# The row maximum of the third stage as a bias of the exponentials, one per head

## The reference

```
h = layernorm(x, ln1_g, ln1_b)
qkv = (h @ Wqkv).reshape(B, S, 16, 24)
q, k, v = qkv[..., :8], qkv[..., 8:16], qkv[..., 16:]
q, k = (rope(q), rope(k))
scores = einsum('bqhd,bkhd->bhqk', q, k) / sqrt(8)
scores = where(causal, scores, -1e9)
probs = softmax(scores, axis=-1)
attn = einsum('bhqk,bkhd->bqhd', probs, v).reshape(B, S, 128) @ Wproj
x = x + attn
```

## Time and profile before

| what | value |
|---|---|
| runs of the kernel before | 4290.12, 4294.4, 4306.48 us; median 4294.4 |
| profiled execution | 4309.58 us, its span 4307.5 us |
| mean granted clock of TensorE | 0.811 of 2.4 GHz |
| PE, DVE, ACT, POOL busy | 2919.2, 2641.8, 1600.9, 1897.7 us of the span |
| L1556, in all stages | 174.3 us in 256 instructions, 681 ns each |
| L1558, in all stages | 177.0 us in 256 instructions, 691 ns each |
| L1259, in all stages | 240.6 us in 384 instructions, 627 ns each |

### The profile page before, as it was taken

One profiled execution on the slowest core, in us unless ns is written; L12 is line 12 of the kernel. 1 busy time (PEld: TensorE's weight loads), 2 busy tenths in 40 slices (PEclk: granted clock), 3 DMA queues, 4 the chain that ended last, 5 costly groups with the idle time before them and its releaser, 6 DMA issues.

```text
span 4307.5 us, 91934 instructions
## 1 busy us (share of the span) xinstructions
PE 2919.2 (68%) x27246; PEld 1985.7 (46%) x27249; DVE 2641.8 (61%) x7148; ACT 1600.9 (37%) x3994; POOL 1897.7 (44%) x2306
## 2 busy tenths in 40 slices
PE   4999998768777777872068878888888770066610
PEld 2666665335444454541046555555555550055510
DVE  2777776447778777874011178888888873044455
ACT  2666665324444444431023244444444440011100
POOL 4222222035565555653720065555555534711167
PEclk9999999967888887875589978888888775588855
DMA  2111111521111111111222110000000001211133
GB/s 52 39 41 38 42 38 37 196 80 40 43 45 38 45 39 39 43 29 37 74 73 75 58 29 24 25 23 26 26 23 24 23 18 45 71 54 54 54 80 87
DMA packets 282376, 207.13 MB, mean 48 GB/s; under 512 B 61730, under 2 KB 246455, under 8 KB 281904
## 3 DMA queue, kind: packets, MB, share of 16 engines
q1 hardware_dynamic: 262960, 164.88, 13.1%
q0 software_dynamic: 19200, 39.62, 3.4%
HBM read 114.99 MB, written 90.18 MB: 48 GB/s over the span
## 4 chain that ended last, share of the span: by engine, by line
PE 20%; DVE 15%; issue 14%; POOL 5%; DVEq 1%; DMA 0%; ACT 0%; POOLq 0%; ACTq 0%
PE scores_ps L1038 3%; PE scores_ps L893 3%; DVE z L1848 2%; POOL rows L2047 2%; DVE row_max L1556 2%; PE scores_ps L902 2%; POOL shared L2144 2%; PE heads_ps L1087 1%; PE scores_ps L1148 1%; PE desk_ps L1045 1%; PE heads_ps L1045 1%; PE turned_ps L908 1%; DVE norm_stat L1534 1%; PE scores_ps L1150 1%; DVE row_max L1837 1%
## 5 line engine op out<-in xcount | busy, mean ns | idle before, releaser
L1991 POOL TENSOR_TENSOR norm_rstd<-norm_veps,minus_half 128x1 f32<-128x1 f32 x384 | 241.2, 628 | 500.7 <-DVE norm_veps L1538 499.8
L1259 ACT ACTIVATE probs<-probs 128x512 f32<-128x512 f32 x384 | 240.6, 627 | 231.3 <-DVE probs L1558 217.7
L2047 POOL DMA_INDIRECT rows<-e_in,slot_put x256 | 249.0, 973 | 163.9 <-issue 107.4
L902 PE MATMUL scores_ps<-consts,probs 128*128 128x128 f32 x1536 | 293.5, 333 | 9.8 <-ACT probs L1259 9.0
L1263 ACT ACTIVATE turned<-scores_ps 128x512 f32<-128x512 f32 x384 | 226.1, 597 | 79.9 <-PE scores_ps L902 70.0
L902 PEld LDWEIGHTS scores_ps<-consts,probs 128*128 128x128 f32 x1536 | 218.2, 172 | 74.4 <-ACT probs L1259 62.5
L1475 DVE TENSOR_REDUCE row_max<-scores_ps 128x8 f32<-128x512 f32 x256 | 174.8, 683 | 63.0 <-PE scores_ps L756 58.1
L1191 ACT ACTIVATE probs<-probs 128x512 f32<-128x512 f32 x256 | 161.4, 630 | 136.3 <-DVE probs L1477 133.9
L1900 DVE COPY shared<-turned_ps 128x256 f32<-128x256 f32 x72 | 30.5, 424 | 266.1 <-PE turned_ps L1140 266.1
L1556 DVE TENSOR_REDUCE row_max<-scores_ps 128x8 f32<-128x512 f32 x256 | 174.3, 681 | 14.6 <-issue 10.1
L1558 DVE TENSOR_TENSOR probs<-scores_ps,row_max 128x512 f32<-128x512 f32 x256 | 177.0, 691 | 8.8
(11 more groups left out here) (338 smaller groups left out, 8772.8 us busy)
## 6 DMA issues: line engine op xcount, KB each, us to landing
hop_dram<-shared SPq DMA_DIRECT2D x64, 256.0 KB, 2.1
hop_in<-hop_dram SPq DMA_DIRECT2D x64, 256.0 KB
rows<-zero_rows SPq DMA_DIRECT2D x64, 144.0 KB, 1.9
shared<-rows SPq DMA_DIRECT2D x72, 128.0 KB, 2.1
moe<-shared SPq DMA_DIRECT2D x72, 128.0 KB, 1.9
rows<-zero_rows SPq DMA_DIRECT2D x64, 128.0 KB, 1.8
c_in<-in_ctx SPq DMA_DIRECT2D x128, 64.0 KB, 2.3
c_two<-in_ctx SPq DMA_DIRECT2D x128, 64.0 KB
```

The lines of the kernel that those rows point to most:

```text
L902: last = pe.transpose(scores_ps[:, a, g, P * k:P * k + P], probs[a][:, P * hp:P * hp + P], ident)
L1259: act.activation(half, half, ACT.Exp, scale=scale).then_inc(at.exped.sem, 1)
L1991: pool.tensor_tensor(n_rstd[:, k, u, :], n_veps[:, k, u, :], minus_half[:, 0:1], ALU.pow).then_inc(sig.sem, 1)
L2047: pool.indirect_dma_start(out=rows, out_offset=bass.IndirectOffsetOnAxis(ap=slot_put[:, c, U * n + i:U * n + i + 1], axis=0), in_=put_rows ...
```

## The change

In the third stage VectorE no longer subtracts. After the maximum of each half it multiplies the eight maxima by minus the scale into a new SBUF tile `low_max` of 128x16 (`best5`). ScalarE makes, instead of one exponential of 512 columns in place, eight of 64 columns (`exp_heads`), one a head, which read the score bank and take that head's column of `low_max` as the bias: exp(scale * s - scale * max). The signals are counted as before: two from VectorE and one from ScalarE a half. Half 0's maximum waits, besides for the scores, for the exponentials of the tile before, since `low_max` is one tile. The later stage keeps `shift5` and `exp5`.

```diff
--- before.py
+++ after.py
@@ -155,6 +155,7 @@
         turned, probs = both("turned", H * S), both("probs", H * S)
         k_bd, v_bd = both("k_bd", H // NR * P), both("v_bd", 8 * NB * 2 * (HD + 1))
         row_max, recip = both("row_max", H), both("recip", H)
+        low_max = sb("low_max", [P, H])
         pad_T = sb("pad_T", [P, NB * (S + 2)])
         stat, mv, veps, rstd = both("stat", 6), both("mv", 2), both("veps", 1), both("rstd", 1)
         minus_half = sb("minus_half", [P, 16])
@@ -1258,6 +1259,14 @@
                 half = probs[a][:, 512 * g:512 * g + 512]
                 act.activation(half, half, ACT.Exp, scale=scale).then_inc(at.exped.sem, 1)
 
+            def exp_heads(at, a, n, g):
+
+                after(act, at.shift.of(n, at.shift.per // 2 * (g + 1)))
+                for h in range(8 * g, 8 * g + 8):
+                    last = act.activation(probs[a][:, S * h:S * h + S], scores_ps[:, a, g, S * (h - 8 * g):S * (h - 8 * g) + S], ACT.Exp,
+                                          scale=SCALE, bias=low_max[:, h:h + 1])
+                last.then_inc(at.exped.sem, 1)
+
             def copy5(at, a, n, g):
                 after(act, at.turned.of(n, g + 1))
                 act.activation(turned[a][:, 512 * g:512 * g + 512], scores_ps[:, a, g, :], ACT.Identity)\
@@ -1278,7 +1287,7 @@
                     act.activation(h_T[1 - u], desk_ps[:, 0:P], ACT.Identity, scale=f_col[:, 0:1], bias=f_col[:, 1:2])\
                        .then_inc(xn_copied.sem, 1)
                 if live(i - 2):
-                    exp5(a3, 1, i - 2, 0, SCALE)
+                    exp_heads(a3, 1, i - 2, 0)
                 if live(i - 1):
                     after(act, f_values.of(i - 1))
                     copy_values5(v_bd[1 - u], 0).then_inc(f_v_copied.sem, 1)
@@ -1307,7 +1316,7 @@
                     act.activation(x_T[u], desk_ps[:, 0:P], ACT.Identity, scale=f_col[:, 2:3], bias=f_col[:, 3:4])\
                        .then_inc(h_copied.sem, 1)
                 if live(i - 2):
-                    exp5(a3, 1, i - 2, 1, SCALE)
+                    exp_heads(a3, 1, i - 2, 1)
                 if live(i - 4):
                     after(act, f_logits.of(i - 4))
                     act.activation(logits0[:, bass.ds(i - 4, 1), :].rearrange("p t e -> p (t e)"), desk_ps[:, 0:8], ACT.Identity)\
@@ -1558,6 +1567,12 @@
                 dve.tensor_tensor(probs[a][:, 512 * g:512 * g + 512].rearrange("p (h t) -> p h t", t=S), sc,
                                   best.unsqueeze(2).broadcast_to([P, 8, S]), ALU.subtract).then_inc(at.shift.sem, 1)
 
+            def best5(at, a, n, g):
+                best = row_max[a][:, 8 * g:8 * g + 8]
+                dve.tensor_reduce(best, scores_ps[:, a, g, :].rearrange("p (h t) -> p h t", t=S), AX, ALU.max).then_inc(at.shift.sem, 1)
+                after(dve, at.shift.of(n, 2 * g + 1))
+                dve.tensor_scalar(low_max[:, 8 * g:8 * g + 8], best, -SCALE, None, ALU.mult).then_inc(at.shift.sem, 1)
+
             def rope5(sig, u):
                 qk = heads_ps[:].rearrange("p (g r n) -> p r g n", g=2, n=P)
                 for k, (dst, table) in enumerate(((rope_c, "cos"), (rope_s, "sin"))):
@@ -1617,8 +1632,8 @@
                 u, j4 = j % U, j % 4
                 half4 = (j // 4) % 2
                 if live(i - 2):
-                    after(dve, a3.score.of(i - 2))
-                    shift5(a3, 1, i - 2, 0)
+                    after(dve, a3.score.of(i - 2), a3.exped.of(i - 3))
+                    best5(a3, 1, i - 2, 0)
                 if live(i - 3):
                     divide5(a3, 1, i - 3)
                 if live(i):
@@ -1638,7 +1653,7 @@
                     dve.tensor_copy(csum4[1 - half4][:], mix_ps[:, 0:4 * MH])
                     dve.tensor_tensor(g_key4[:], in_gate4[:], mix_ps[:, 0:4 * MH], ALU.subtract).then_inc(block_done.sem, 1)
                 if live(i - 2):
-                    shift5(a3, 1, i - 2, 1)
+                    best5(a3, 1, i - 2, 1)
                 if live(i - 3):
                     after(dve, f_out.of(i - 3), r4_added.of(i - 5))
                     dve.tensor_tensor(y[1 - u], heads_of[1][:, 256:384], x2_ring[(j - 3) % 4], ALU.add).then_inc(f_norm.sem, 1)
```

## The result

The changed kernel takes 4363.1 us (median of 4 runs, 4345.7 to 4374.4) against 4300.4 us for the kernel before on the same chip (4 runs, 4290.1 to 4318.4): 1.0132 times as long, interval 1.0103 to 1.016, that is 57 us more (44 to 69; the two medians alone lie 63 apart). It is slower, as forecast, but by nearly twice the 30 us. The profiled execution took 4374.4 us, with a span of 4372.5. (In the experiments, one run of the kernel before on the chip of e1 to e4 was a slow one, 6037 us, and is left out of their ratios.)

What follows compares the result with a forecast made beforehand. No engine was full; chains between engines bounded the third stage. First half 10.6 plus second half 19.5 made 30 us on the 4294.4 us median: 4324 us (+0.7%), own range 4309 to 4340, stated range 4296 to 4364.

Steps and rivals of the forecast that it cites:

- The price of eight ACTIVATEs: ScalarE's eight exponentials a half: 1.70 us by the trace's bias pair (q_ring, k_raw), 1.08 more than the one before.
- First half, 10.6 us: First turning 0.32 us late in short periods, 1.07 with a table load, hidden in slow ones; 10.6 us over 64 tiles.
- Second half, 19.5 us: Everything behind ScalarE's second exponential 1.08 us late; 7 periods pay 1.08, 14 pay 0.46; 19.5 us over 64 tiles.
- the sum's 0.62 of cover: TensorE's wait for xn at L1007 in the slow period, taken off the 1.08 us lateness, leaving 0.46.
- rival (2): TensorE's longer mid-period idle gap lowers its granted clock, so short periods become slow: 4339 to 4365 us; chance 0.20.
- (3): Rival: ScalarE's eight exponentials do not overlap and take 2.44 us, giving 4363 us; chance 0.12.
- The prediction's own sign for it: Third stage's mean granted clock off 0.81 by more than 0.03 would make rival (1) or (2) the story.
- VectorE's gain, 0: Second half: VectorE's 0.5 us saved is lost waiting at cmax for GpSimd's spread of keys; gain 0.
- (1): Rival: TensorE's second-half lateness heals itself through a higher clock before the first turning; some 4300 us; chance 0.20.
- (4): Rival: VectorE was the bound and cmax is not held, so the kernel gets faster, 4273 us; chance 0.06.
- The signs forecast for waits and busy time: L1007's wait for xn shrinks, VectorE's wait at L1599 grows, VectorE's busy time falls some 64 us.
- One term at the upper bound: First half, eight taking 2.44 us: five slow periods with a table load pay 0.75 us each.

Runs made afterwards that it cites:

- e1: Kernel before with only the first half of the third stage changed to eight biased exponentials: 1.0005 of the kernel before.
- e4: Changed kernel plus five unread 256-column TensorE products a period, ahead of the second turning: 1.0115 of the kernel before.
- e2: Kernel before with only the second half of the third stage changed to eight biased exponentials: 1.0145 of the kernel before.
- e10: Changed kernel plus three unread 512-column TensorE products a period, all behind the second turning: 0.997 of the kernel before.
- e8: Kernel before plus two unread 512-column ScalarE exponentials ahead of the second half's own: 1.0112 of the kernel before.
- e7: Changed kernel plus three unread 512-column TensorE products a period, two ahead of the second turning, one behind: 0.9975 of the kernel before.
- e3: Changed kernel with one 512-column exponential a half, biased by the first head's maximum: 0.9955 of the kernel before.
- e5: Changed kernel with one maximum over the whole half and one 512-column exponential biased by it: 0.9966 of the kernel before.
- e6: Changed kernel with four 128-column exponentials a half, each under its first head's maximum: 0.9967 of the kernel before.

## Why the prediction was right and wrong

**The price of eight ACTIVATEs: right.** 1.70 us was forecast, 1.74 measured. The Trainium skill ("ScalarE: Activation LUTs", What ACT_TABLE_LOAD costs) gives 2.01 as an estimate. For one instruction the trace agrees with its formula (333 ns measured and worked out), but the eight overlap by more than its 93 ns: 1.74 us is a step of 0.20 us. Going by the row of the bias pair was better.

**First half, 10.6 us: the lateness was right, its price was not shown.** The turning is 0.36 us late in the short period, against 0.32. The step that fails is "the lateness is paid in full, and VectorE's 0.3 to 0.5 us gained is spent waiting for the squares". I followed VectorE to L1599 and passed over its rope_s, for which GpSimd's two sums ahead of h_rstd (L2017, L2018) wait. In the period of e1 shown above the two cancel. Its interval (9 us less to 14 more) would still hold 10.6, but the rows show the same start of the spread.

**Second half, 19.5 us: the step that failed.** e2 measured 62 us (44 to 80). The lateness was sized rightly (1.08 us; TensorE's idle time there measured 1.08 on average), and so was its place. What the sum put at nothing is that TensorE's own work then takes longer: the four groups took 4.75 us on average instead of 3.62, and L893 was slow in 63 of 64 executions instead of 30. That used up nearly all of L1007's wait, and the sum's 0.62 of cover with it. This was rival (2), the gap that costs clock, given 0.20 and 4339 to 4365; the median of 4363 lies at its far end, and outside the forecast's own 4309 to 4340. The stated range, up to 4364, holds it by 1 us, and only because rivals (2) and (3) set its upper end. The direction was forecast for a reason that held; the size was not, and that the range holds it is in part luck. The rival's wording is too narrow too: it laid the clock to the one gap ahead of the second turning, and in e10 that gap stands while the clock is 0.85. The prediction's own sign for it, a granted clock off 0.81 by more than 0.03, came (0.72). e8 shows that lateness alone brings it, e7 and e10 that the time comes back with the clock although the lateness stays. The forecast's sum held the durations of the earlier trace rows fixed, although the same rows showed L989 at 0.66 us in one period and at 1.11 in the next.

**VectorE's gain, 0: right at cmax, wrong in all.** cmax is held until the spread's end (1448.59 against 1448.57). But the half I did not follow gives 15 to 19 us when ScalarE isn't made late (e3, e5). So the cost of the eight exponentials is larger than the 57 us: against e3, which differs from the changed kernel in them alone, it is 1.0132 - 0.9955, 1.8 per cent or 76 us.

**The other rivals.** (1) Healing did not happen: the slow matmuls came on top of TensorE's lateness. (3) The eight do overlap (1.74 us), so its 4363, near the median, has the wrong cause. (4) Faster through VectorE: the gain exists, by another path, and is too small here. The signs forecast for waits and busy time came: L1007's wait nearly gone, the variance's grown, VectorE less busy (2641.8 to 2615.2 us), though by 27 and not by 64: the 128 scalings of 0.23 us give some 30 back, which leaves 59, and cmax takes 16 more (63 x 0.25 us); the other 16 are open. One term at the upper bound is 0.71 and not 0.75 (1.81 - 1.1), which changes its sum by 0.3 us.

## What to carry to other kernels

A delay that makes TensorE wait can have two prices: the delay itself, which the next wait may cover, and the longer durations of everything behind it where the granted clock falls, which may use that cover up. So beside "who waits how long" ask at which of its two clocks each group of TensorE ran, and make the sum also with all of them at the slow one. When an engine is relieved, follow each of its results to its reader, not only the last in its list: here the gain came through GpSimd. And a per-head bias that splits one 512-column ACTIVATE into eight of 64 columns costs 1.1 us; where a shift common to several heads will do, one instruction keeps VectorE's gain, and four seem to. (e6's four take the first head's maximum of each pair; a kernel for use would need that of the pair, which was not run.)

## What the runs showed of the hardware

- The 512-column exponential from PSUM with a bias column took 0.68 us (e5), against 0.61 to 0.63 for the one from and to SBUF; eight of 64 columns 1.74, four of 128 columns 1.13.
- Between e5 and the changed kernel the granted clock of the stage went from 0.82 to 0.72, with e6 between (0.78), but the ratio moved clearly only in the last step: 0.9966, 0.9967, 1.0132 (intervals of some 0.2 per cent to each side).
- Three bf16 products of 512 columns a period, 0.59 us for two and 0.38 for one in the rows of e7, brought the mean clock of the stage from 0.72 to 0.86, and the kernel with more work on TensorE ran 68 us faster by the ratios.
- GpSimd's spread of 1.90 us held VectorE's cmax until its own end: 0.55 to 0.59 us instead of 0.16 to 0.18 in 35 of 63 periods of the changed kernel (2 before), 465 ns on average against 217:

```profile
L1665 DVE TENSOR_TENSOR cmax<-csum,row_max 128x8 f32<-128x8 f32 x63 | 29.3, 465 | 0.0
```
